# A mixture-of-experts kernel: TensorE's expert loop with seven passes through its branches ahead of the first expert, and its inner loop rotated

## What is computed

```
probs = softmax(xr @ Wg);  gate_vals, expert_idx = top_k(probs, 2)
C = 640                                     # capacity of an expert, in tokens
dispatched = xr[...]                        # (8, C, 512): each expert's tokens
h = relu(einsum('ecd,edf->ecf', dispatched, w1))   # hidden size 2048
expert_out = einsum('ecf,efd->ecd', h, w2)
out = sum over the two choices of gate * expert_out, added to x
```

## Time and profile before

| | |
|---|---|
| median of three runs | 1264.4 us (1262.67 to 1265.08) |
| the profiled execution | 1265.84 us, its span 1263.7 us |
| PE busy | 1051.8 us (83%) |
| DVE busy | 693.6 us (55%) |
| ACT busy | 527.8 us (42%) |
| POOL busy | 306.5 us (24%) |
| first matmul of expert 0 | 474.75 us |
| last write into the output | 1257.27 us |

### The profile page before, as it was taken

How to read it: one execution, slowest core, us unless ns; L and a number is a source line. 1 busy time by engine, 2 the same in 40 slices (tenths; PEclk the granted TensorE clock), 3 DMA queues, 4 the chain that set the end, 5 groups by cost and what they waited for, 6 DMA issues and landing times.

```text
span 1263.7 us, 16714 instructions
## 1 busy us (share of the span) xinstructions
PE 1051.8 (83%) x5058; PEld 830.8 (66%) x5059; DVE 693.6 (55%) x1026; ACT 527.8 (42%) x845; POOL 306.5 (24%) x251
## 2 busy tenths in 40 slices
PE   1045886886899719999999999999897997999994
PEld 0022343433457519998999899889786886988883
DVE  6989899899872523334333433445454343333553
ACT  5354645835844202334233333334454333333453
POOL 4767727547530230001000200020202002000202
PEclk9998897987998759999999999999998998999997
DMA  7151150111021351114311622253535135211721
GB/s 245 39 160 34 65 182 32 67 68 66 0 82 43 145 202 68 66 67 127 89 66 66 151 101 97 103 115 133 157 130 171 66 133 140 69 66 66 189 87 20
DMA packets 63420, 125.53 MB, mean 99 GB/s; under 512 B 4726, under 2 KB 4762, under 8 KB 63384
## 3 DMA queue, kind: packets, MB, share of 16 engines
q1 hardware_dynamic: 54728, 107.91, 24.5%
q0 software_dynamic: 8656, 17.13, 6.7%
HBM read 93.04 MB, written 35.22 MB: 101 GB/s over the span
## 4 chain that ended last, share of the span: by engine, by line
PE 57%; issue 4%; ACT 1%; POOL 0%; DVE 0%; DVEq 0%; ACTq 0%; POOLq 0%
PE ps_h L1099 9%; PE ps_h L1101 9%; PE ps_y L1110 9%; PE ps_h L1100 9%; PE ps_y L1111 9%; PE ps_y L1112 9%; PE ps_t L1073 1%; POOL out_dram L1052 0%; ACT xh L1209 0%; ACT y L1216 0%; ACT w1h L1181 0%; DVE w1l L1232 0%; DVEq L1154 0%; DVE hl L1271 0%; DVEq L105 0%
## 5 line engine op out<-in xcount | busy, mean ns | idle before, releaser
L1099 PE MATMUL ps_h<-xh,w1h 128*128 128x320 f32 (+3 forms) x768 | 250.7, 326 | 38.2 <-issue 36.3
L1101 PE MATMUL ps_h<-xh,w1l 128*128 128x320 f32 (+3 forms) x768 | 246.3, 321 | 0.0
L1100 PE MATMUL ps_h<-xl,w1h 128*128 128x320 f32 (+3 forms) x768 | 246.2, 321 | 0.0
L1271 DVE SCALAR_TENSOR_TENSOR hl<-ps_h,hh 128x320 fp32r<-128x320 f32 (+1 forms) x192 | 107.0, 558 | 229.0 <-ACT hh L1205 224.3
L1052 POOL DMA_INDIRECT out_dram<-y,token x40 | 63.2, 1579 | 692.2 <-ACT y L1216 514.9
L1110 PE MATMUL ps_y<-w2h,hh 128*128 128x512 f32 (+1 forms) x528 | 206.8, 392 | 1.0 <-DVE hl L1271 1.0
L1111 PE MATMUL ps_y<-w2h,hl 128*128 128x512 f32 (+1 forms) x528 | 206.8, 392 | 0.0
L1112 PE MATMUL ps_y<-w2l,hh 128*128 128x512 f32 (+1 forms) x528 | 206.0, 390 | 0.0
L1205 ACT ACTIVATE hh<-ps_h 128x320 fp32r<-128x320 f32 (+1 forms) x192 | 94.3, 491 | 266.8 <-PE ps_h L1101 266.6
L1235 DVE TENSOR_TENSOR w2l<-raw,w2h 128x512 fp32r<-128x512 f32 x128 | 88.5, 692 | 198.0 <-ACT w2h L1184 197.1
L428 PE MATMUL ps_mm<-r1T,wm 128*128 (+1 forms) x320 | 162.3, 659 | 21.3 <-ACT z_in L590 14.4
(11 more groups left out here) (190 smaller groups left out, 1291.4 us busy)
## 6 DMA issues: line engine op xcount, KB each, us to landing
raw<-in_L_ffn_w_dram SPq DMA_DIRECT2D x64, 1024.0 KB
slots<-r_rows SPq DMA_DIRECT2D x8, 1302.5 KB, 15.2
rows<-slots SPq DMA_DIRECT2D x8, 1302.5 KB, 9.1
f_rows<-in_fside_BxSxS_dram SPq DMA_DIRECT2D x5, 1024.0 KB, 5.4
rows<-in_x_dram SPq DMA_DIRECT2D x4, 1024.0 KB, 6.2
out_dram<-x_rows SPq DMA_DIRECT2D x4, 1024.0 KB, 5.3
slots<-r_rows POOLq DMA_DIRECT2D x1, 1302.5 KB
rows<-slots SPq DMA_DIRECT2D x5, 260.5 KB, 3.9
```

Source lines behind the costliest of these rows:

```text
L1099: nc.tensor.matmul(o, w1h[:, j, dt, :], xh[:, dt, lo:hi], start=(dt == 0), stop=False)
L1100: nc.tensor.matmul(o, w1h[:, j, dt, :], xl[:, dt, lo:hi], start=False, stop=False)
L1101: last = nc.tensor.matmul(o, w1l[:, j, dt, :], xh[:, dt, lo:hi], start=False, stop=(dt == CT - 1))
L1271: v.scalar_tensor_tensor(out=hl[:, j % 2, lo:hi], in0=ps_h[:, bank, 0:hi - lo], scalar=0.0, in1=hh[:, j % 2, lo:hi].bitcast(F32), op0=ALU.max,
```

## The change

Four things change.

1. `visit_counts`, a new table of 64 numbers: the seven widths, then each expert's count at place 7, 8, 16, 24, ..., 56. Seven memsets of one column on VectorE write the widths, early in the first block, and two small copies behind `counts` write the rest.
2. On TensorE the turns of the first rows no longer stand ahead of the expert loop. Inside it stands a second loop over visits. For expert 0 it has eight rounds: in the first seven a width is read from the table, the tree of branches goes to that width's leaf, and there a branch leads past the expert's code to the end. The eighth makes the five turns and then goes to the leaf of expert 0's true width, where the code is run. For the other experts the loop has one round.
3. The body, now `expert(e, n)`, is written with the loop rotated: up(2q), down(2q-1) except in the first round, up(2q+1), down(2q), the turn; the last down stands behind the loop. The matmuls run in the same order as before, the turns after the same `down`, but one copy of `up` fewer stands in the code of each width.
4. Both kinds of body wait for the preceding expert's last `hl` in one wait ahead of the loop; the bodies above 512 tokens had two waits, one for each half.

In the same count, the visit loop now begins at 1143 (the expert loop around it at 1142), the tree at 1192, the leaves at 1195 (256), 1376 (320), 1582 (384), 1787 (448), 2018 (512), 2247 (576) and 2550 (640), and all jump to 2851. The last instruction is 2857. The second block began at 1556 before and begins at about 1138 now; the first block's code is the same.

```diff
+WIDTHS = range(2 * P, CAP + 1, P // 2)
+VISITS = len(WIDTHS)
...
+        for n, width in enumerate(WIDTHS):
+            v.memset(visit_counts[:, n:n + 1], width)
...
         v.tensor_scalar(counts[:], ps_count, 1.0, float(CAP), ALU.max, ALU.min).then_inc(s_count, 1)
         dve.wait_ge(s_count, 2)
+        v.tensor_copy(visit_counts[:, VISITS:VISITS + 1], counts[:, 0:1])
+        v.tensor_copy(visit_counts[:, VISITS + 1:].rearrange("p (e v) -> p e v", v=VISITS + 1)[:, :, 0], counts[:, 1:])
...
-        def up(hidden, j, n, first=False):
+        def up(hidden, j, n):
...
-                    pe.wait_ge(s_hl, 2 * hidden + (2 if first else 0))
+                    pe.wait_ge(s_hl, 2 * hidden)
...
+        def expert(e, n):
+            pe.wait_ge(s_cur_h, e + 1)
+            pe.wait_ge(s_cur_l, e + 1)
+            pe.wait_ge(s_hl, 2 * FT * e + 2)
+            pe.nop(nofuse=True)
+            with pe.Fori(0, FT // 2) as q:
+                at = e * FT + q * 2
+                up(at, 0, n)
+                with pe.If(q > 0):
+                    down(at - 1, 1, n)
+                up(at + 1, 1, n)
+                with pe.If(q < 1):
+                    pe.wait_ge(s_ya, e + 1)
+                    pe.wait_ge(s_yv, e + 1)
+                    down(at, 0, n, first=True)
+                with pe.Else():
+                    down(at, 0, n)
+                with pe.If(q < TURN_FROM):
+                    pe.nop(nofuse=True)
+                with pe.Else():
+                    turn_one_of(e, q, 0, ST + 1)
+            down(e * FT + (FT - 1), 1, n, last=True)
+
         pe.sem_inc(s_f, 2)
-        for i in range(ST):
-            first_turn(i)
         with pe.Fori(0, NE) as e:
-            count = pe.value_load(counts[0:1, bass.ds(e, 1)], min_val=1, max_val=CAP)
...
+            with pe.Fori(e * (VISITS + 1), VISITS + 1) as visit:
+                count = pe.value_load(visit_counts[0:1, bass.ds(visit, 1)], min_val=1, max_val=CAP)
+                with pe.If(visit < VISITS):
+                    pe.nop(nofuse=True)
+                with pe.Else():
+                    with pe.If(e < 1):
+                        for i in range(ST):
+                            first_turn(i)
+                    with pe.Else():
+                        pe.nop(nofuse=True)
+
+                def choose(widths):
+                    if len(widths) == 1:
+                        with pe.If(visit < VISITS):
+                            pe.nop(nofuse=True)
+                        with pe.Else():
+                            expert(e, widths[0])
+                        return
```

More of the change, by code:

```diff
@@ L83, in build_program @@
         counts = sb("counts", [P, NE], I32)
+        visit_counts = sb("visit_counts", [P, (VISITS + 1) * NE], I32)
         rows = sb("rows", [P, ST, ROW])
@@ L100, in build_program @@
         with ExitStack() as phase:
-            conditioning_and_routing(nc, phase, ident, counts, rows, cond_buffers, gate_parts, place0, load_sems,
+            conditioning_and_routing(nc, phase, ident, counts, visit_counts, rows, cond_buffers, gate_parts, place0, load_sems,
                                      slots, out_rows, x, fside, cond, w1c, u1c,
@@ L105, in build_program @@
         with ExitStack() as phase:
-            experts(nc, phase, ident, counts, rows, place0, load_sems, slots, out_rows, w1, w2)
+            experts(nc, phase, ident, counts, visit_counts, rows, place0, load_sems, slots, out_rows, w1, w2)
 def load_chunk(sp, sem, raw1, raw2, w1, w2, e, c):
@@ L120, in first_pieces, with conditioning_and_routing @@
             [(raw2[:, 0, 0], w2h[:, 0], w2l[:, 0], 1)])
-def conditioning_and_routing(nc, ctx, ident, counts, rows, cond_buffers, gate_parts, place0, load_sems,
+def conditioning_and_routing(nc, ctx, ident, counts, visit_counts, rows, cond_buffers, gate_parts, place0, load_sems,
                              slots, out_rows, x, fside, cond, w1c, u1c,
@@ L942, in _, with experts @@
             v.tensor_tensor(low, raw, high.bitcast(F32), ALU.subtract).then_inc(load_sems[3 + 2 * which], 1)
-def experts(nc, ctx, ident, counts, rows, place0, load_sems, slots, out_rows, w1, w2):
+def experts(nc, ctx, ident, counts, visit_counts, rows, place0, load_sems, slots, out_rows, w1, w2):
     def sb(name, shape, dt=F32):
@@ L978, in experts @@
     HALF = CAP // 2
-    CLASSES = range(2 * P, CAP + 1, P // 2)
     TURN_FROM = 2
@@ L1078, in turn_one_of @@
             if last == first + 1:
-                turn(e, first)
+                if first < ST:
+                    turn(e, first)
+                else:
+                    pe.nop(nofuse=True)
                 return
@@ L1115, in _ @@
         pe.sem_inc(s_f, 2)
-        for i in range(ST):
-            first_turn(i)
         with pe.Fori(0, NE) as e:
-            count = pe.value_load(counts[0:1, bass.ds(e, 1)], min_val=1, max_val=CAP)
[L1121 to L1131, removed]
-                    with pe.Else():
[L1133 to L1138, removed]
-                    with pe.Else():
[L1140 to L1151, removed]
@@ new lines, in _ @@
+            with pe.Fori(e * (VISITS + 1), VISITS + 1) as visit:
[6 more added lines that the diff above has]
+                            first_turn(i)
+                    with pe.Else():
+                        pe.nop(nofuse=True)
+                def choose(widths):
+                    if len(widths) == 1:
+                        with pe.If(visit < VISITS):
+                            pe.nop(nofuse=True)
+                        with pe.Else():
+                            expert(e, widths[0])
+                        return
+                    middle = (len(widths) - 1) // 2
+                    with pe.If(count < widths[middle] + 1):
+                        choose(widths[:middle + 1])
+                    with pe.Else():
+                        choose(widths[middle + 1:])
+                choose(WIDTHS)
```

## The result

The changed kernel takes 1308.84 us (median of 4 runs, 1305.9 to 1311.17) against 1264.51 us for the one before (4 runs, 1262.67 to 1265.08): a ratio of 1.0362, 95% interval 1.0333 to 1.0391. It is slower by 44 us. The forecast was 1292.3 us, and the range, up to 1312, holds the time.

A forecast was written before the change was run, and what follows sets the result against it. From 475 us on TensorE was taken as the bound, with stops for code fetches. Visits +38.9, later entries -8.2 and clock -2.8 gave +27.9 us on 1264.4: 1292.3 us, range 1262 to 1312.

The forecast's parts named there:

- Visits ahead of expert 0: TensorE's seven visits: 16.8 us of own instructions and six stops, 31.5 us; expert 0 starts 38.9 us later.
- The later entries: First matmuls of experts 3 to 7: stops gone at some, new at others, 8.2 us gained in sum.
- the clock: TensorE is granted half speed behind a stop; fewer stops behind expert 0's start gain 2.8 us.
- Expert 3, 4 and 5 find their blocks: Their code is still held at entry, so their stops go: 2.9, 3.9 and 5.6 us gained.
- A stop in the way of expert 6: Block 11 is gone at expert 5's end; a 5.2 us gap replaces 8.90, 3.7 us gained.
- the rule: TensorE's code sits in eight ring places of 256-instruction blocks; arriving fetches a missing next block, a missing target stops the sequencer.
- nine blocks for eight places: The new loop fills eight blocks and its end has one more fetched, so blocks are thrown out: six stops in the visits.
- Rotated loop and joined wait: TensorE's expert body: same matmuls, one more branch a round, costs nothing; with an expert's longer head, range 0 to 3 us.
- VectorE's small work: Seven memsets and two small copies in the first block: nothing, at worst 1 us.
- B, the code stays: Rival: visits stop only twice, all later stops go; 7.7 us faster, 1256.7 us; chance 0.12.
- C, seven stops and none later: Rival: a stop in each visit, none at later experts; 16.4 us slower, 1280.8 us; chance 0.20.
- D: Rival: nothing is warmed, each visit stops twice, experts as before or worse; about 1353 us; chance 0.02.

The follow-up runs named there:

- experiment 4: The changed kernel with all seven visits, moved 178 instructions on by 87 transposes that are jumped over: 1271.48 us, ratio 1.0067 to the kernel before.
- 9: The changed kernel, not moved, with five widths and five visits in place of seven: 1262.82 us, ratio 0.9993 to the kernel before.
- experiment 1: The kernel before with the rotated loop but without the visits: 1260.63 us, ratio 0.9937 to the kernel before.
- experiment 8: The changed kernel moved 178 instructions on by jumped-over transposes, with each of the seven visits made twice: 1289.76 us, ratio 1.0185 to the kernel before.
- 5: The kernel before, moved 124 instructions on by 60 transposes that are jumped over: 1264.08 us, ratio 1.001 to it unmoved.
- experiment 6: The rotated loop without visits, moved 150 instructions on by 75 small products that TensorE executes: 1239.98 us, ratio 0.9801 to the kernel before.
- 10: The kernel before, moved 144 instructions on by 72 small products that TensorE executes: 1244.1 us, ratio 0.9843 to it unmoved.
- 11: The rotated loop without visits, with five widths in place of seven, not moved: 1234.74 us, ratio 0.9776 to the kernel before.
- experiment 2: The kernel before, moved 144 instructions on by 70 transposes that are jumped over: 1257.06 us, ratio 0.9908 to it unmoved.
- experiment 3: The rotated loop without visits, moved 154 instructions on by 75 transposes that are jumped over: 1246.15 us, ratio 0.985 to the kernel before.
- experiment 7: The changed kernel, not moved, with each of the seven visits made twice: 1341.16 us, ratio 1.0591 to the kernel before.
- 12: The rotated loop without visits, with five widths, moved 168 instructions on by 84 small executed products: 1234.49 us, ratio 0.9763 to the kernel before.

## Why the prediction was right, and where it was not

*Visits ahead of expert 0* (+38.9 us forecast, +40.7 measured, +44.0 from the meeting point on). Right in kind, 5.2 us too small. Own instructions 17.3 us for 16.8, stops 34.6 for 31.5: seven for six, 4.9 us each for 5.25. Which visits stop was not right: 448 passes, and 320 and 640 stop, because of the wrong positions. The rest, some 1.6 us, is what the forecast had at nothing between the meeting point and the turns: the loops' heads (455.2 to 455.8 us) and the eighth round's own load and branches (507.7 to 508.9). That the profiles differ by 40.7 only is luck, the meeting point of the second one 3.3 us earlier. That the visits don't use the idle time is right: they begin at 455.8 us, behind the meeting point.

*The later entries* (-8.2) *and the clock* (-2.8). This is the step that failed: a gain of 11.0 us was forecast, and 0.6 us were lost. "Expert 3, 4 and 5 find their blocks" was wrong: they stood still for 5.73, 5.75 and 2.26 us. "A stop in the way of expert 6" was wrong the other way: 0.21 us. The long one at the end of expert 6 came (12.45 us, for the 8.90 I took). The cause is the count of positions, not the rule: with them right, the rule puts the stops where they are, and experiments 4 and 9 show that the gain is there (28.7 us from expert 0 on) as soon as no ninth block passes through. So nine blocks for eight places, on which the forecast stood, is shown; which of them are thrown out hangs on borders that I had misplaced. The time stayed in the range because that allowed for it: "later entries with no gain" was priced there at 11 us more. (In the same sentence six stops of 3.5 us take 31.5 - 21 = 10.5 us off, not 9.5.)

The clock follows the gaps: behind the stop of 12.45 us TensorE was granted 0.71 for 6 us and 1.00 in the 6 us behind them. Windows of the changed kernel, busy us (count) by engine and then the granted clock, at expert 7:

```profile
1222.95:1228.95 6.00, 6.00 (x28) 5.84 (x29) 1.63 (x3) 2.19 (x5) 0.38 (x2) 0.71 0.13 21
1228.95:1234.95 6.00, 6.00 (x34) 5.03 (x33) 3.52 (x6) 2.89 (x6) 0.00 (x0) 1.00 0.00 0
```

28 multiplications for 34: 1.1 us lost, less than the 1.9 us that the forecast took behind a long stop.

*Rotated loop and joined wait* (nothing). Right for the rotation: experiment 1 has expert 0 at 475.5 for 474.75 and is not slower than before. The longer head of an expert, with its second loop, is not quite hidden: 1.40 and 1.36 us under "issue" at experts 4 and 5 in experiment 4. From expert 0 on that kernel takes 760.9 us, the five widths without visits 1230.4 - 470.88 = 759.5: 1.4 us in all, within the 0 to 3 given. *VectorE's small work*: nothing to be seen of it.

*The sum.* +27.9 forecast; between the two profiled spans it is 1305.1 - 1263.7 = +41.4, of which 1.8 are missing in the visits and 11.6 in the later entries and the clock. The other 2.9 us to the medians' 44.3 are in how each profiled execution stands to its median (1.3 us above it before, 1.5 below it now), and the 3.3 us of the meeting point are enough for them. Counted from the meeting point, the visits are 5.2 us short and the later entries and the clock 11.6, together 16.8 us for the 16.4 between forecast and medians.

*The rivals.* B, the code stays, needed no more than 3.8 stops; there were seven. C, seven stops and none later, came close for the visits (42.8 us for 44.0) and had the rest wrong. D is far off. The rule of two blocks in the Trainium skill ("Runtime: NRT & Kernel Launch", "Instruction fetch mechanics") fails again by a run: in experiment 8 seven visits go through seven blocks without one packet. The Trainium skill's block of 256 instructions, in the same section, agrees with the packets, and TensorE's 128 KiB, by division eight blocks of 16 KiB, is the number of places with which the rule gives the packets of before, of the changed kernel and of experiments 4, 5, 6, 8, 9, 10 and 11.

*Open.* Why block 8 was fetched at the first entry into block 7 in experiment 4, and not in the profiles of 2 and 3, the traces don't show; experiment 6 avoids it and does not explain it. Nor is it shown which stops the faster executions of experiment 1 leave out, or where the 48th packet of experiment 7 comes from.

## What to carry to other kernels

If a profile shows waits under "issue" at the first entries of a loop's branches, lay the packets of the code queue beside the positions of the code and count the blocks of the loop, with the one behind its end. Here seven blocks had no stop behind expert 0 (9, 11 and 12), eight had none (4), one (6) or four (1) by the order of the entries, and nine had four (before) or one long one (10). Less code or code moved to other borders takes stops away (here 1.6 to 2.4%), and it costs nothing where it is hidden in idle time; a walk through the code beforehand pays for every block itself, on the path that it was to clear, unless TensorE would be idle there anyway (a walk placed in idle time was not run). Count positions against the trace's own rows before leaning on them: one kind of instruction counted wrong moved every border.

## What the runs showed that I had not expected

- The place of unchanged code is worth 1.6%: moved by 144 instructions that do work in idle time, 1244.1 us for 1263.1; moved by 124, jumped over, no difference.
- The same kernel can have two times, 10 to 15 us apart (experiment 2: 1244.6 and 1257 to 1260; experiment 3: 1241.4 and 1251 to 1253). The profiles of slower ones have extra fetches and stops at expert 1; that the faster ones lack them is argued from experiments 6 and 10, which have one time each, not seen.
- A neighbouring block that is wanted right behind a stop costs nearly a full stop again (4.29 us), though it is the block that is fetched behind anyway.
